# One TensorE signal for a quad of chunks, or two, in a graph kernel of gathers and one-hot sums

## The chip, the cores and the metric

The kernel runs on one core of a Trainium2 chip. The metric is the time of one execution on the device, in microseconds (us). Changes are judged against runs of the kernel before.

## The reference

A block of a graph network on 3125 nodes with 256 features and 53125 directed edges. `src`, `dst` and the edge weights are inputs, so where an edge reads and adds is only known at run time. Cut to what matters:

```python
h = relu(layernorm(x))
x_fwd = segment_sum(w * h[dst, :128], src) / max(degree(src), 1)
x_bwd = segment_sum(w * h[src, 128:], dst) / max(degree(dst), 1)
x = x + concat(x_fwd, x_bwd)

def gat_layer(x, W, b, a, g, beta):
    h = x @ W.T + b
    score = (h @ a[:d])[src] + (h @ a[d:])[dst]
    e = exp(-leaky_relu(score, 0.2))
    return layernorm(segment_sum(e[:, None] * h[dst], src)) * g + beta

h = relu(layernorm(x))
heads = concat([elu(gat_layer(h, ...)) for 8 heads of width 64])   # width 512
x = x + elu(gat_layer(heads, ...))                                 # width 256
```

All of it is in float32.

## The kernel before

Nodes lie in 25 tiles of 128. The kernel sorts the edges by the tile of the node they are summed into, in 464 chunks of 128 edges; two chunks are a group, which belongs to one tile, and four chunks are a quad (116 quads). Sixteen slots hold the rows of sixteen chunks (four quads, a round; 29 rounds).

There are four passes over all chunks. The first (order S) and the second (order D) make the two halves of the weighted mean. The last two are the attention passes "1" (8 heads, rows of 520 numbers) and "2" (one head, rows of 257). In each the same is done for every chunk: GpSimd gathers 128 rows of a table in HBM into the chunk's slot with an indirect DMA (`gather`, L433); TensorE multiplies a one-hot matrix of "edge to lane in its tile" with the rows, so that the rows of one node are added up in PSUM; VectorE adds the finished sum of a group to the accumulator of its tile (`add_group`, L1163, whose add is L1166).

*First and second pass.* ScalarE multiplies the gathered rows by the edge weights (`scale_rows`, L550), VectorE makes a quad's one-hots (`one_hots`, L1158), TensorE sums the quad (`sum_rows`, L809 to L819: four matmuls, two for each group, shown as two records each), VectorE adds (`add_sums`, L1168). Beside 42 of the first 52 quads of a pass, and again in the first pass behind its second cut (`CUT`, quad 56), the sort of the next part of the edges goes on: VectorE makes one-hots of a batch of ten columns of edges (`place_batch`, L1130 to L1137), ScalarE more of them (L538, L541), TensorE 40 matmuls (`place`, L803 to L806), of which the last signals `col_free`, for which the second next batch waits (L1130). The second pass has such batches only until quad 52: what comes behind its second cut is called its tail here.

The signal that binds these is `chunks_summed`, raised by one by TensorE's matmul of every chunk. Three places wait for it: the gather of chunk c for chunk c - 16 (its slot is free), VectorE's one-hots of a quad for the quad four back, and VectorE's adds for their own quad. TensorE in turn waits for `sum_free`, which VectorE's adds raise: a quad is summed when the adds of the quad three back are done.

*Attention passes.* In the order of one turn (quad q), each engine in program order:

- TensorE (`turn`, L955): `source_scores` of quad q + 1 (12 small matmuls, L935; they need the transposed one-hots that ScalarE copied), then `transposed` of quad q + 2 (4 transposes, L925; they need ScalarE's one-hots), then `sums` of quad q (4 matmuls, L950).
- VectorE (`turn`, L1423): `messages` of q (four operations, L1413 in pass 1, L1411 in pass 2), `scores` of q + 1 (L1398, then the leaky ReLU L1402), `add_groups` of q - 1 (L1166).
- ScalarE (`turn`, L650): `weights` of q + 1 (the exponential, L647), the copy of the transposed one-hots of q + 2 (L643), `one_hots` of q + 3 (four of L634, one of L638).
- GpSimd (`gather_layer1`, L447): the gather of chunk c waits in pass 1 for VectorE's message of chunk c - 16, in pass 2 for the sum of its group (`sum_ready`).

TensorE signals four times a quad here: `ohT_psum` after the transposes (ScalarE's copy waits), `ssrc_ready` after the source scores (VectorE's scores wait), and `sum_ready` after each of two groups (VectorE's adds, ScalarE's one-hots, and the gathers of pass 2 wait).

The order on each engine is the order of the program as written. The wait of a gather is the code's line

```python
pool.wait_ge(chunks_summed, phase * CHUNKS + c + 1)
```

where `chunks_summed` begins at 16.

## Time and profile before

| | |
|---|---|
| median of 3 runs | 3293.55 us (3287.83 to 3297.24) |
| the profiled execution | 3294.2 us |
| its span, first to last instruction | 3292.4 us |
| mean granted TensorE clock | 0.825 |
| busy share: PE, DVE, ACT, POOL | 68%, 58%, 53%, 59% |
| gathers | 4 x 464 |

PE is TensorE, PEld its weight loads, DVE VectorE, ACT ScalarE, POOL GpSimd. A line such as L818 is a line of the kernel before. In a row of the timeline the last bracket is how long the engine had been idle before the instruction, and what ended that; "remote" is a releaser that the profile doesn't know, "issue" means that it saw nothing to wait for. The ends of matmuls are modelled. The clock is given as a share of full speed.

### The profile page before, as it was taken

The page shows a single profiled execution, that of the slowest core. Times are in us where ns is not written, and L with a number is a line of the kernel's source. Part 1 is how long each engine was busy: PE and PEld are TensorE (multiplying, and loading weights), DVE is VectorE, ACT ScalarE, POOL GpSimd, SP SyncE. Part 2 cuts the span into 40 slices and gives each one's busy share as a digit, 9 for nine tenths or more (in the row PEclk, how much of TensorE's full clock was granted, in tenths as well). Part 3 has the DMA queues.
Part 4 walks back from the last instruction along what each step waited for, and adds up shares of the span by engine and source line. Part 5 has one row for each costly group of instructions (what it writes and reads, how often), then busy time and mean ns, then how long its engine had stood idle before and what let it go on. Part 6 is the DMA issues. An engine that isn't in the chain of part 4 may idle for free. (4 is left out here: it accounts for less than half of the span.)

```text
span 3292.4 us, 46358 instructions
## 1 busy us (share of the span) xinstructions
PE 2243.2 (68%) x14916; PEld 1669.3 (51%) x14916; DVE 1917.8 (58%) x4213; ACT 1738.7 (53%) x5133; POOL 1928.0 (59%) x1999
## 2 busy tenths in 40 slices
PE   6887778677758877343577777777767566655653
PEld 4785667567747766233343333333335445444542
DVE  8985788577747776222446666666686233333336
ACT  3995677578747776222334444344438344444444
POOL 1006666666666666666635656665645566666664
PEclk8998999799878999555688888888888777777776
DMA  2011111111141112111545656665641333333335
GB/s 60 1 41 40 40 44 43 43 45 45 45 47 44 45 44 53 47 46 47 58 140 160 169 164 173 169 170 157 168 104 33 87 92 89 91 89 90 90 90 77
DMA packets 114882, 270.48 MB, mean 82 GB/s; under 512 B 34543, under 2 KB 51670, under 8 KB 114646
## 3 DMA queue, kind: packets, MB, share of 16 engines
q0 software_dynamic: 89088, 245.53, 30.5%
q1 hardware_dynamic: 25558, 21.98, 2.1%
q8 instruction: 126, 2.06, 0.3%
q14 instruction: 110, 0.90, 0.1%
HBM read 250.96 MB, written 16.42 MB: 81 GB/s over the span
## 5 line engine op out<-in xcount | busy, mean ns | idle before, releaser
L435 POOL DMA_INDIRECT rows_near<-table_a,s_idx_S x464 | 474.1, 1022 | 286.0 <-issue 115.4
L435 POOL DMA_INDIRECT given<-table,s_idx_S x464 | 449.2, 968 | 301.5 <-issue 126.8
L1166 DVE TENSOR_TENSOR work<-work,bank 128x129 f32 (+2 forms) x928 | 391.0, 421 | 362.4 <-remote 163.1
L435 POOL DMA_INDIRECT rows_near<-table,s_idx_S x464 | 446.8, 963 | 252.7 <-issue 127.8
L435 POOL DMA_INDIRECT rows_near<-table_b,s_idx_D x464 | 450.0, 970 | 230.9 <-issue 101.9
L950 PE MATMUL bank<-scratch,oh 128*128 128x512 f32 x928 | 488.1, 675 | 15.9 <-DVE scratch L1413 11.7
L818 PE MATMUL bank<-rows_near,oh 128*128 128x129 f32 x1856 | 331.0, 330 | 246.6 <-issue 179.5
L647 ACT ACTIVATE e_att<-lrelu 128x32 f32<-128x32 f32 (+1 forms) x232 | 49.9, 215 | 740.6 <-DVE lrelu L1402 490.0
L818 PEld LDWEIGHTS bank<-rows_near,oh 128*128 128x128 f32 x1856 | 289.0, 234 | 282.1 <-issue 232.8
L935 PE MATMUL bank<-sort_ring,scratch 128*128 x2784 | 154.0, 169 | 329.4 <-ACT scratch L643 285.2
L538 ACT ACTIVATE scratch<-scratch,given 128x128 f16<-128x128 bf16 x840 | 284.1, 388 | 170.8 <-DVE scratch L1130 146.7
L935 PEld LDWEIGHTS bank<-sort_ring,scratch 128*128 128x128 bf16 x2784 | 135.8, 100 | 455.3 <-issue 436.5
L538 ACT ACTIVATE sort_ring<-sort_ring,given 128x128 f16<-128x128 bf16 x840 | 284.1, 388 | 132.2 <-DVE sort_ring L1130 110.2
L950 PEld LDWEIGHTS bank<-scratch,oh 128*128 128x128 f32 x928 | 193.2, 219 | 224.8 <-issue 204.3
L634 ACT ACTIVATE scratch<-iota_f,s_lo_S 128x128 f32<-128x128 f32 x928 | 293.4, 389 | 18.3 <-PE bank L906 13.7
L803 PE MATMUL bank<-scratch 128*128 128x224 bf16 (+1 forms) x840 | 228.9, 273 | 100.2 <-ACT scratch L538 68.7
L803 PE MATMUL bank<-rows_near,sort_ring 128*128 128x224 bf16 (+1 forms) x840 | 227.7, 271 | 76.2 <-ACT sort_ring L538 50.7
L550 ACT ACTIVATE rows_near<-rows_near,s_w_D 128x128 f32<-128x128 f32 x464 | 163.0, 394 | 216.8 <-DMA rows_near<-table_b,s_idx_D 190.5
L805 PE MATMUL bank<-scratch 128*128 128x224 bf16 (+1 forms) x840 | 229.2, 273 | 15.8 <-issue 15.5
L806 PE MATMUL bank<-scratch 128*128 128x224 bf16 (+1 forms) x840 | 229.3, 273 | 13.6 <-issue 13.6
L804 PE MATMUL bank<-scratch 128*128 128x224 bf16 (+1 forms) x840 | 229.2, 273 | 9.8 <-issue 9.8
L805 PE MATMUL bank<-rows_near,sort_ring 128*128 128x224 bf16 (+1 forms) x840 | 227.6, 271 | 8.3 <-issue 8.1
(222 smaller groups left out, 4799.8 us busy)
## 6 DMA issues: line engine op xcount, KB each, us to landing
rows_near<-table_a,s_idx_S POOLq DMA_INDIRECT x464
rows_near<-table_b,s_idx_D POOLq DMA_INDIRECT x464
rows_near<-table,s_idx_S POOLq DMA_INDIRECT x464
given<-table,s_idx_S POOLq DMA_INDIRECT x464
table<-scratch SPq DMA_DIRECT2D x25, 260.0 KB
table<-scratch SPq DMA_DIRECT2D x25, 128.5 KB, 3.0
xs<-in_x SPq DMA_DIRECT2D x1, 3072.0 KB
out_x<-scratch SPq DMA_DIRECT2D x24, 128.0 KB, 1.7
```

What stands on the lines that cost most here:

```text
L435: nc.gpsimd.indirect_dma_start(out=to, out_offset=None, in_=table[:, :], in_offset=bass.IndirectOffsetOnAxis(ap=s_idx[order][:, c:c + 1], ...
L538: last = nc.scalar.activation(oh_row[n % RING][:, j, :], oh_lane[n % RING][:, j, :], ACT.Copy, scale=row_mid_f[o][:, c:c + 1])
L550: nc.scalar.activation(rows0[:, slot, 0:HALF], rows0[:, slot, 0:HALF], ACT.Copy, scale=s_w[o][:, c:c + 1]).then_inc(rows_scaled, 1)
L634: last = nc.scalar.activation(off_by[:, side + k, :], iota_f[:, 0:P], ACT.Abs, scale=-1.0, bias=s_lo["S"][:, bass.ds(q * QUAD + k, 1)])
L803: nc.tensor.matmul(high, oh_w[n % RING][0][:, j, :], chunks, start=start, stop=stop, skip_group_check=True)
L804: nc.tensor.matmul(low, oh_w[n % RING][1][:, j, :], chunks, start=False, stop=stop, skip_group_check=True)
L805: nc.tensor.matmul(node, oh_node[n % RING][:, j, :], chunks, start=start, stop=stop, skip_group_check=True)
L806: last = nc.tensor.matmul(row, oh_row[n % RING][:, j, :], chunks, start=False, stop=stop, skip_group_check=True)
L818: nc.tensor.matmul(sum0(g), oh[:, slot, :], rows0[:, slot, :], start=(k % GP == 0), stop=(k % GP == GP - 1)).then_inc(chunks_summed, 1)
L935: last = nc.tensor.matmul(bank[2 + u % 2][:, k * heads:(k + 1) * heads], ohT[:, u % 2, k * P:(k + 1) * P], s_parts[:, f, bass.ds(tiles[k / ...
L950: mm = nc.tensor.matmul(bank[4 + u % 2 * 2 + k // GP][:, 0:width], lanes, rows, start=(k % GP == 0), stop=(k % GP == GP - 1))
L1166: v.tensor_add(a, a, psum).then_inc(sum_free[o], 1)
```

## The change

TensorE's signals are made coarser, and every wait for them is rewritten to count quads.

- First and second pass: `chunks_summed` becomes `quads_summed`, raised by the last of a quad's four matmuls. It begins at 4. A gather waits only if it is a quad's first, and then for the whole quad four back; the other three of a quad carry no wait. VectorE's one-hots and adds wait for the same events as before.
- Attention passes: `ohT_psum` and `ssrc_ready` become one signal, `turned_and_scored`, given behind the transposes (of quad q + 2), which come after the source scores (of quad q + 1). So VectorE's scores now wait for the transposes too. `sum_ready` is given once, by the quad's last matmul; VectorE's first add of a quad waits for both groups, and in pass 2 a gather waits for both groups of the quad four back.

No instruction of an engine changes its place. Cut to its core:

```diff
                 for c in range(CHUNKS):
...
-                    pool.wait_ge(chunks_summed, phase * CHUNKS + c + 1)
+                    if c % QUAD == 0:
+                        pool.wait_ge(quads_summed, phase * QUADS + c // QUAD + 1)
                     gather(table, rows0[:, c % SLOTS, 0:HALF], order, c)
...
-                        pool.wait_ge(sum_ready[o], (c - SLOTS) // GP + 1)
+                        pool.wait_ge(sum_ready[o], (c - SLOTS) // QUAD + 1)
...
                 def transposed(q, u):
-                    act.wait_ge(ohT_psum[o], q + 1)
+                    if isinstance(q, int) and q < 2:
+                        act.wait_ge(turned_and_scored[o], q + 1)
+                    else:
+                        act.wait_ge(turned_and_scored[o], q + 2)
...
-                                act.wait_ge(sum_ready[o], i * (2 * UNROLL) + 2 * u)
+                                act.wait_ge(sum_ready[o], i * UNROLL + u)
...
-                    nc.tensor.matmul(sum0(g), oh[:, slot, :], rows0[:, slot, :],
-                                     start=(k % GP == 0), stop=(k % GP == GP - 1)).then_inc(chunks_summed, 1)
+                    last = nc.tensor.matmul(sum0(g), oh[:, slot, :], rows0[:, slot, :],
+                                            start=(k % GP == 0), stop=(k % GP == GP - 1))
+                last.then_inc(quads_summed, 1)
...
-                        if k % GP == GP - 1:
-                            mm.then_inc(sum_ready[o], 1)
+                    last.then_inc(sum_ready[o], 1)
...
-                            source_scores(i * UNROLL + (u + 1), u + 1, tiles[2 * u:2 * u + 2])
-                        if not isinstance(i, int) or q + 2 < QUADS:
-                            transposed(i * UNROLL + (u + 2), u + 2)
+                            last = source_scores(i * UNROLL + (u + 1), u + 1, tiles[2 * u:2 * u + 2])
+                            if not isinstance(i, int) or q + 2 < QUADS:
+                                last = transposed(i * UNROLL + (u + 2), u + 2)
+                            last.then_inc(turned_and_scored[o], 1)
                         sums(q, u)
...
-                dve.wait_ge(chunks_summed, phase * CHUNKS + q * QUAD + QUAD)
+                dve.wait_ge(quads_summed, phase * QUADS + q + 1)
...
-                dve.wait_ge(chunks_summed, SLOTS + phase * CHUNKS + QUAD * (q + 1))
+                dve.wait_ge(quads_summed, SLOTS // QUAD + phase * QUADS + q + 1)
...
-                    dve.wait_ge(ssrc_ready[o], q + 1)
+                    dve.wait_ge(turned_and_scored[o], q + 3)
...
                 def add_groups(q, u, tiles):
+                    dve.wait_ge(sum_ready[o], q + 1)
                     for j in range(2):
-                        dve.wait_ge(sum_ready[o], q * 2 + (j + 1))
```

## Rows read from the trace of the kernel before

**Rows 1.** The page: its span, and the granted TensorE clock in 40 slices.

```profile
span 3292.4 us, 46358 instructions
...
PEclk8998999799878999555688888888888777777776
```

**Rows 2.** Busy time by stage: length, PE, PEld, DVE, ACT, POOL, clock, DMA, GB/s.

```profile
255.50:605.00 349.50, 269.77 (x2185) 229.81 (x2185) 259.37 (x467) 242.61 (x812) 228.29 (x224) 0.92 0.17 43
605.00:962.50 357.50, 258.94 (x2171) 232.17 (x2172) 241.22 (x412) 247.44 (x823) 245.77 (x240) 0.89 0.23 44
962.50:1302.00 339.50, 258.79 (x2118) 224.71 (x2118) 232.00 (x376) 244.53 (x818) 222.27 (x225) 0.91 0.20 45
1302.00:1642.00 340.00, 141.86 (x538) 113.47 (x539) 97.79 (x272) 96.67 (x247) 226.81 (x239) 0.54 0.27 50
1697.00:2439.00 742.00, 558.74 (x2702) 271.55 (x2703) 476.39 (x916) 302.35 (x800) 453.69 (x464) 0.85 0.61 166
2561.00:3240.00 679.00, 408.01 (x2720) 319.70 (x2721) 230.82 (x936) 296.21 (x794) 440.29 (x463) 0.76 0.36 90
```

**Rows 3.** Waits in the tail, 1330 to 1597 us: total, times, longest.

```profile
DVE work L1166 <- remote: 129.8, 27, 8.1
```

**Rows 4.** Timeline of the tail: start, length, instruction, idle before it.

```profile
1392.44 2.40 PE L818 MATMUL bank<-rows_near,oh 128*128 128x129 f32 x8 [1.51 <-issue]
...
1397.30 0.95 POOL L435 DMA_INDIRECT rows_near<-table_b,s_idx_D  x1 [0.30 <-issue]
...
1398.76 0.94 POOL L435 DMA_INDIRECT rows_near<-table_b,s_idx_D  x1 [0.52 <-issue]
...
1400.75 0.72 DVE L1166 TENSOR_TENSOR work<-work,bank 128x129 f32 x2 [7.82 <-remote]
1400.88 0.95 POOL L435 DMA_INDIRECT rows_near<-table_b,s_idx_D  x1 [1.17 <-remote]
...
1401.58 2.06 PE L818 MATMUL bank<-rows_near,oh 128*128 128x129 f32 x8 [6.73 <-issue]
...
1403.70 0.95 POOL L435 DMA_INDIRECT rows_near<-table_b,s_idx_D  x1 [1.88 <-PE bank L818]
...
1456.12 0.95 POOL L435 DMA_INDIRECT rows_near<-table_b,s_idx_D  x1 [0.47 <-remote]
...
1457.55 0.94 POOL L435 DMA_INDIRECT rows_near<-table_b,s_idx_D  x1 [0.48 <-issue]
```

**Rows 5.** Waits before any gather, 100 to 250 us.

```profile
DVE sort_ring L1130 <- PE bank L806: 9.2, 14, 1.0
```

**Rows 6.** Waits in the first attention pass, 1700 to 2430 us.

```profile
DVE score L1398 <- remote: 179.1, 39, 18.0
```

**Rows 7.** Timeline of the first attention pass.

```profile
2009.84 0.45 PE L935 MATMUL bank<-sort_ring,scratch 128*128 x12
...
2015.52 0.95 POOL L435 DMA_INDIRECT given<-table,s_idx_S  x1 [0.30 <-issue]
2018.84 0.19 DVE L1398 TENSOR_TENSOR score<-bank,given 128x32 f32<-128x32 f32 x1 [7.00 <-remote]
```

**Rows 8.** Waits in the second attention pass, 2565 to 3240 us.

```profile
DVE score L1398 <- remote: 303.5, 48, 11.3
...
DVE score L1398 <- PE bank L935: 54.2, 34, 3.3
```

**Rows 9.** Timeline of the second attention pass.

```profile
2709.08 0.16 DVE L1398 TENSOR_TENSOR score<-bank,given 128x4 f32<-128x4 f32 x1 [0.92 <-PE bank L935]
2709.18 0.72 ACT L638 ACTIVATE oh<-scratch,ones 128x512 f32<-128x512 f32 x1
...
2709.96 0.61 PE L925 MATMUL bank<-ident_bf,oh 128*128 128x128 bf16 x4 [0.91 <-ACT oh L638]
...
2710.60 0.60 ACT L643 ACTIVATE scratch<-bank 128x512 bf16<-128x512 bf16 x1 [0.61 <-PE bank L925]
2711.10 1.27 ACT L634 ACTIVATE scratch<-iota_f,s_lo_S 128x128 f32<-128x128 f32 x4
```

More of the change, by code:

```diff
@@ L313, in build @@
         gathered = [sem(f"gathered{i}") for i in range(SLOTS)]
-        chunks_summed = sem("chunks_summed")
+        quads_summed = sem("quads_summed")
         oh_ready = {o: sem(f"oh_ready_{o}") for o in "SD12"}
@@ L317, in build @@
         sum_free = {o: sem(f"sum_free_{o}") for o in "SD12"}
-        ohT_psum = {o: sem(f"ohT_psum_{o}") for o in "12"}
+        turned_and_scored = {o: sem(f"turned_and_scored_{o}") for o in "12"}
         ohT_ready = {o: sem(f"ohT_ready_{o}") for o in "12"}
-        ssrc_ready = {o: sem(f"ssrc_ready_{o}") for o in "12"}
         off_made = {o: sem(f"off_made_{o}") for o in "12"}
@@ L925, in transposed @@
                         last = nc.tensor.transpose(turned[u % 2][:, k * P:(k + 1) * P], upper, ident_bf[:, :])
-                    last.then_inc(ohT_psum[o], 1)
+                    return last
                 def source_scores(q, u, tiles):
@@ L937, in source_scores @@
                                                     start=(f == 0), stop=(f == 2))
-                    last.then_inc(ssrc_ready[o], 1)
+                    return last
                 def sums(q, u):
@@ L949, in sums @@
                             lanes, rows = m[:, 0:P], row_slots(u * QUAD + k, 1)[:, 0, 0:width]
-                        mm = nc.tensor.matmul(bank[4 + u % 2 * 2 + k // GP][:, 0:width], lanes, rows,
-                                              start=(k % GP == 0), stop=(k % GP == GP - 1))
-                        if k % GP == GP - 1:
-                            mm.then_inc(sum_ready[o], 1)
+                        last = nc.tensor.matmul(bank[4 + u % 2 * 2 + k // GP][:, 0:width], lanes, rows,
+                                                start=(k % GP == 0), stop=(k % GP == GP - 1))
+                    last.then_inc(sum_ready[o], 1)
                 def turn(i):
@@ L960, in turn @@
                         if not isinstance(i, int) or q + 1 < QUADS:
-                            source_scores(i * UNROLL + (u + 1), u + 1, tiles[2 * u:2 * u + 2])
-                        if not isinstance(i, int) or q + 2 < QUADS:
-                            transposed(i * UNROLL + (u + 2), u + 2)
+                            last = source_scores(i * UNROLL + (u + 1), u + 1, tiles[2 * u:2 * u + 2])
+                            if not isinstance(i, int) or q + 2 < QUADS:
+                                last = transposed(i * UNROLL + (u + 2), u + 2)
+                            last.then_inc(turned_and_scored[o], 1)
                         sums(q, u)
-                transposed(0, 0)
-                transposed(1, 1)
-                source_scores(0, 0, tile_numbers(mybir.EngineType.PE, "S", TILE_AT, 2))
+                transposed(0, 0).then_inc(turned_and_scored[o], 1)
+                transposed(1, 1).then_inc(turned_and_scored[o], 1)
+                source_scores(0, 0, tile_numbers(mybir.EngineType.PE, "S", TILE_AT, 2)).then_inc(turned_and_scored[o], 1)
                 turn(0)
@@ L1019, in _ @@
             dve.sem_inc(consts_made, 1)
-            dve.sem_inc(chunks_summed, SLOTS)
+            dve.sem_inc(quads_summed, SLOTS // QUAD)
             dve.sem_inc(col_free, RING)
```

## The prediction

> **What bounds the kernel now.** I read the page first [rows 1]: a span of 3292.4 us in an execution of 3294.2 us, and a granted TensorE clock that sits at half speed in slices 17 to 20 and well under full after them, which says that TensorE waits. So I cut the span into stages [rows 2]: the first pass until its second cut (349.5 us), its rest (357.5), the second pass while edges are still being placed (339.5), its tail (340.0), and the two attention passes (742 and 679).
>
> In each stage I ask how fast the gathers alone could go. Between two gathers that nothing delays GpSimd idles 0.30 us [rows 4], so a stage's floor is its GpSimd busy time plus 0.30 us for each gather [rows 2]. Tail: 226.8 + 239 x 0.30 = 298.5 us of 340.0. First attention pass: 453.7 + 464 x 0.30 = 592.9 of 742. Second: 440.3 + 139.2 = 579.5 of 679. The first three stages: 228.3 + 245.8 + 222.3 + 689 x 0.30 = 903 of 1046.5. So 41, 149, 99 and 143 us are stalls of the gathers, on a ring of 16 slots. Something behind the ring is late.
>
> What is late? In the tail, VectorE's adds of finished sums idled 129.8 us in 27 waits put down to "remote", a releaser the profile can't name [rows 3]. They wait for TensorE's signal alone, and for their own previous add. The timeline shows such a wait [rows 4]: TensorE's eight matmuls (a chunk is two records) ran from 1392.44 us to 1394.84, and TensorE did nothing until 1401.58; VectorE had been idle 7.82 us when it started at 1400.75. All matmuls issued so far had ended 5.9 us before. **The signal of a finished matmul arrives microseconds late.** In those microseconds GpSimd issued gathers back to back (1397.30, 0.30 us after the one before), and the wait ended just when GpSimd had to pause (0.52, then 1.17 us idle). Elsewhere in the tail GpSimd goes in lockstep, 0.47 or 0.48 us idle before each gather [rows 4], 0.17 more than undisturbed. In the stretch before any gather runs, the same handover from TensorE to VectorE costs 9.2 us in 14 waits, 1.0 at most [rows 5]. My reading: while GpSimd issues gathers, TensorE's signals queue up, and get through mainly when GpSimd pauses.
>
> Both attention passes show it. In the first, `score` waited 179.1 us in 39 "remote" waits; the small matmuls it needs began at 2009.84 and take under half a microsecond, the last gather before the pause was issued at 2015.52, and `score` began at 2018.84 after 7.00 us idle [rows 6, 7]. In the second it is 303.5 us in 48 waits [rows 8]. GpSimd then runs out of slots and TensorE idles.
>
> **The change, part by part.** The instructions of the engines stay in their order. TensorE's signals fall from four to one per quad in the first two passes (928 to 232) and from four to two in the attention passes (928 to about 466).
>
> *Signals themselves.* Eight records with four signals take 2.06 us at half clock [rows 4], about 0.22 a start, so a signal shows no time of its own: 0. The Trainium skill (TensorE: Matmul & The Clock Gate, "The cost: per-tile semaphore tail") says increments serialise at about 26.3 ns each; by it the 1,158 removed would give an estimated 30 us at most, and none where TensorE waits. No row here shows that cost by itself, and the rule has no delay of microseconds in it, which this trace does have.
>
> *Tail of the second pass.* At four signals per quad and four gathers per quad, one signal gets through per pause of 0.17 us. With one signal a quad, GpSimd pauses once in four: 60 quads x 0.17 = 10 us of stall remain of 41. I take **-30**; ends 0 and -41.
>
> *Coarser wait of the gathers.* The first gather of a quad now waits for the fourth chunk of the quad four back, not its first: up to three quarters of 2.06, 1.5 us, where it was the wait that ended last. Chunks two to four lose their waits. A row speaks against a cost: the gather at 1403.70, released by L818, began after all eight records of 1401.58 had ended (1403.64) [rows 4]. Late signals come in bunches. I take 0 in the tail; ends 0 and 1.5 us x 116 quads = +174 a pass.
>
> *First three stages.* A batch of 40 placing matmuls with one signal of its own sits in most steps, and VectorE's next batch waits for that signal, which the change leaves alone. VectorE is busy 259 of 349.5 us there, TensorE 270 [rows 2]. I take **-5** of 143.
>
> *First attention pass.* Signals per quad go from four to two, half a signal per gather: a held signal has fewer in front of it. The stall to be had is 149 us. TensorE's work is 558.7 us / 116 = 4.8 us a quad and VectorE's 4.1, against the gathers' 5.1 [rows 2], so none forbids a gain. But what holds the signals is GpSimd's gathers, and these remain as dense. I take a quarter: **-35**; ends +20 and -130.
>
> *Second attention pass.* The same quarter of 99 is -25. Against it: the scores' signal now comes after the transposes too, which wait for ScalarE's one-hots. A row shows the distance: `score` at 2709.08, one-hots at 2709.18 for 0.72, the transposes at 2709.96 for 0.61 [rows 9], so 1.5 us later. It costs where VectorE waits for exactly that, 34 times [rows 8]: 51 us if nothing absorbs it. Since the ring and not the single quad bounds the pass I charge 15: **-10**; ends +80 and -80. In the first attention pass `score` comes after four messages of VectorE that cover most of it.
>
> *VectorE's adds* wait for both groups of a quad at once; their sums are a quad old by then: 0.
>
> Sum: -30 - 5 - 35 - 10 = -80, so 3294.2 - 80 = **3214 us**. The profiled execution is 0.65 us above the median of the runs (3293.55), so nothing is to be corrected.
>
> **The rivals.** *The hold hardly counts the signals.* It ends when GpSimd pauses and lets all through, however many there are. For it: the long waits shown end with GpSimd's long pauses, not its short ones [rows 4, 7]. Then only the tail gains, the attention passes do not, and the later scores signal takes something back: 3294 - 30 + 15 = 3279. Chance 0.22.
>
> *The queue was all of it.* With fewer signals than pauses nothing piles up, and the passes go near their floors: -38 in the tail, -110 and -70 in the attention passes, -35 before: 3041. For it: lockstep one to one in the tail. Against it: the batch signal of the first stages is already rare. Chance 0.15.
>
> *Slower: the merged signal.* The signal of scores and transposes closes a loop: `score` and its leaky ReLU, weights, the copy of the transposes (0.60), one-hots (1.27 and 0.72 us on ScalarE), transposes (0.61), `score` [rows 9]. It decides once that loop with a held signal exceeds the 5.1 us of four gathers; with some 0.6 us for the three small ones that comes to 3.8 us without a hold, so a mean hold over 1.3 us per quad is enough. If it takes 1.5 us at half of the 232 attention quads (174 us) and pauses of the ring hide 80 of that, then with the tail's gain the time is 3294 + 174 - 80 - 30 = 3358. Chance 0.10; and 0.05 that the coarser gather wait costs half a quad's matmuls (1 us) at 100 of 232 quads, 3294 + 100 - 45 = 3349.
>
> *Nothing moves*: the signals still arrive with the next pause of GpSimd, and all that goes is a price per signal, for which no row shows more than nothing: 3294. Chance 0.04. (By the skill's rule quoted above this case would give 3264.)
>
> **How the numbers follow.** Forecast 0.44, rivals 0.22, 0.15, 0.15 (two slower ones) and 0.04. A measurement of this kernel tells about 0.3%, or 10 us, from no change. The first rival lies at the edge of that: I give 0.15 of its 0.22 to faster and 0.07 to no change. Faster 0.44 + 0.15 + 0.15 = 0.74, plus 0.02 from slower ones that gain elsewhere: 0.76. Same 0.07 + 0.04 = 0.11. Slower 0.13. The forecast's own terms reach from 3294 - 41 - 15 - 90 - 50 = 3098 to 3294. The range 3100 to 3310 leaves out most of the full relief (0.13) and the slower cases beyond 3310 (0.09).
>
> **What would show it.** In the changed profile: the tail near 310 us, GpSimd's 0.47 us pauses rarer and single; VectorE's "remote" waits of the adds well under 129.8 us; `score`'s 179.1 and 303.5 us reduced by a quarter or more; the granted clock at half speed over fewer slices. Direct waits of `score` for TensorE should grow in the second attention pass, now ended by the transposes. It is wrong if the attention passes keep 742 and 679 us, or if the second one grows.

## The result, and the profile after

The changed kernel takes 3301.43 us (median of 18 runs, 3287.80 to 3309.49), the kernel before beside it 3290.25 us (18 runs, 3278.86 to 3297.24). The ratio is 1.0029, with a 95% interval of 1.0016 to 1.0042. The forecast was 3214 us, 80 us less than before; not only was nothing gained, some 10 us were lost. All lines of this document are lines of each run's own kernel, so that one statement can have several numbers: the adds are L1166 before and L1170 in the changed kernel.

The page of the changed kernel, its span and the granted clock, to be laid beside [rows 1]:

```profile
span 3289.2 us, 46126 instructions
...
PEclk8997999899978998555688889888887777777776
```

Busy time by stage over the same windows and in the same columns as [rows 2]:

```profile
255.50:605.00 349.50, 273.35 (x2200) 233.81 (x2201) 263.89 (x483) 243.87 (x815) 232.51 (x229) 0.90 0.17 44
...
1302.00:1642.00 340.00, 174.93 (x548) 119.03 (x547) 96.63 (x278) 99.73 (x255) 229.09 (x243) 0.55 0.28 51
1697.00:2439.00 742.00, 563.71 (x2704) 271.52 (x2704) 476.28 (x918) 294.70 (x792) 464.68 (x461) 0.85 0.60 166
2561.00:3240.00 679.00, 431.89 (x2727) 332.89 (x2725) 240.07 (x948) 293.65 (x798) 439.32 (x464) 0.76 0.37 90
```

In each window GpSimd gets through nearly the same number of gathers as before (243 in the tail for 239, 461 for 464, 464 for 463), at the same clocks (0.55, 0.85, 0.76 for 0.54, 0.85, 0.76). Nothing sped up anywhere. These windows can't show where the 10 us went: the profiled execution of the changed kernel took 3291.18 us, 3 us less than the profiled one of before.

The waits in the tail, 1330 to 1597 us, in total, times and longest; first GpSimd's own in the kernel before, beside the line of [rows 3]:

```profile
POOL rows_near L435 <- issue: 33.3, 108, 0.5
...
POOL rows_near L435 <- remote: 30.9, 47, 3.2
...
POOL rows_near L435 <- PE bank L818: 23.1, 33, 2.1
```

and the changed kernel:

```profile
DVE work L1170 <- remote: 128.0, 16, 19.0
...
POOL rows_near L434 <- issue: 54.5, 179, 0.3
POOL rows_near L434 <- remote: 28.8, 9, 4.7
```

This is the reading of the whole case. The change did what it says: a gather has to wait for a signal only once a quad, and GpSimd's waits for TensorE fell from 80 (47 remote, 33 direct) to 9. The **sum** of GpSimd's idle time hardly moved, 83.3 us for 87.3. Both windows hold 188 gathers, and 188 x 0.30 = 56.4 us of it is there without any delay, so the delays are 27 us for 31. VectorE's adds tell the same, 128.0 us of remote waits in 16 for 129.8 in 27, the longest now 19.0 us for 8.1. Fewer and longer waits, nearly the same time.

The changed kernel's timeline in the tail shows one such wait. To read it one has to count quads: the first matmuls below are those of quad 70, the records of 1390.28 and 1392.77 those of quad 72, the adds of 1398.62 those of quad 70, and the gather of 1398.75 is the first of quad 74, which waits for quad 70.

```profile
1381.72 2.06 PE L821 MATMUL bank<-rows_near,oh 128*128 128x129 f32 x8 [5.20 <-DVE work L1170]
...
1390.28 2.03 PE L821 MATMUL bank<-rows_near,oh 128*128 128x129 f32 x6 [0.60 <-issue]
...
1392.77 0.80 PE L821 MATMUL bank<-rows_near,oh 128*128 128x129 f32 x2 [0.46 <-issue]
...
1394.75 0.94 POOL L434 DMA_INDIRECT rows_near<-table_b,s_idx_D  x1 [0.30 <-issue]
...
1397.28 0.40 ACT L550 ACTIVATE rows_near<-rows_near,s_w_D 128x128 f32<-128x128 f32 x1 [0.83 <-DMA rows_near<-table_b,s_idx_D]
1398.62 0.72 DVE L1170 TENSOR_TENSOR work<-work,bank 128x129 f32 x2 [7.39 <-remote]
1398.75 0.94 POOL L434 DMA_INDIRECT rows_near<-table_b,s_idx_D  x1 [3.06 <-remote]
...
1399.45 2.06 PE L821 MATMUL bank<-rows_near,oh 128*128 128x129 f32 x8 [5.89 <-DVE work L1170]
```

The last row confirms the count: quad 73 may be summed when the adds of quad 70, three back, are done. So quad 70 was summed at 1383.78 us, and its one signal let VectorE and GpSimd go on at 1398.62 and 1398.75, **14.84 us** later. TensorE had summed two further quads meanwhile, the last at 1393.57, and GpSimd had been out of slots since 1395.69. The trace also keeps the times at which a semaphore was raised. This one rose at 1398.49, 1398.59 and 1398.68, for quads 70, 71 and 72, and then at 1401.53, 0.02 us behind the end of quad 73.

Counted in this way over quads 58 to 107, the adds of a quad begin 10.3 us (median) behind its matmuls in the changed kernel, and 14.0 and 12.0 us in two profiles of the kernel before. Single quads reach 16.7 us in the changed kernel and 19.6 in the kernel before. Behind some long stops of GpSimd (3.06 us at 1398.75) two of the next quads are handed over in 0.15 us, and then the delay is back; behind others (4.24 us at 1477.37) it doesn't go away at all. One signal a quad is held about as long as four were.

In the kernel before, the adds of 1400.75 in [rows 4] are by the same count those of quad 69, summed at 1384.58, 16.17 us earlier. Its semaphore rose nine times between 1403.45 and 1403.79. But it also rose seven times between 1386.5 and 1391.48, while the gathers came 0.30 us apart, each signal 11 to 14 us late. So a pause isn't the only time in which signals pass.

In the attention passes (1700 to 2430 and 2565 to 3240 us, two answers) `score` waits as follows, for 179.1 us in 39 waits [rows 6], and for 303.5 in 48 and 54.2 in 34 [rows 8]:

```profile
DVE score L1402 <- remote: 169.7, 38, 14.4
```

```profile
DVE score L1402 <- remote: 241.8, 56, 14.9
...
DVE score L1402 <- PE bank L929: 121.1, 53, 2.4
```

In the second pass 62 us of remote waits went, and 67 us of direct waits for the transposes came. The pass is as long as before.

### The profile page after: what moved, and what is told of

Same layout as the page of the kernel before. It is cut to its first block and busy times, and to the rows that moved or that the text cites. A ratio compares the mean times of both kernels' runs of the same rounds, so it can differ in the third digit from the quotient of the medians.

```text
span 3289.2 us, 46126 instructions
## 1 busy us (share of the span) xinstructions
PE 2307.1 (70%) x14916; PEld 1694.7 (52%) x14916; DVE 1919.3 (58%) x4213; ACT 1730.4 (53%) x5133; POOL 1941.4 (59%) x1999
## 5 line engine op out<-in xcount | busy, mean ns | idle before, releaser
L434 POOL DMA_INDIRECT rows_near<-table,s_idx_S x464 | 455.0, 981 | 279.3 <-issue 128.3
L1170 DVE TENSOR_TENSOR work<-work,bank 128x129 f32 (+2 forms) x928 | 390.1, 420 | 368.0 <-remote 176.2
L821 PE MATMUL bank<-rows_near,oh 128*128 128x129 f32 x1856 | 367.2, 337 | 225.8 <-DVE work L1170 76.1
L821 PEld LDWEIGHTS bank<-rows_near,oh 128*128 128x128 f32 x1856 | 296.9, 231 | 289.1 <-issue 187.6
L806 PE MATMUL bank<-scratch 128*128 128x224 bf16 (+1 forms) x840 | 230.3, 274 | 94.3 <-ACT scratch L538 54.1
L806 PE MATMUL bank<-rows_near,sort_ring 128*128 128x224 bf16 (+1 forms) x840 | 229.1, 273 | 67.4 <-ACT sort_ring L538 39.5
L808 PE MATMUL bank<-scratch 128*128 128x224 bf16 (+1 forms) x840 | 230.6, 274 | 16.5 <-issue 16.5
L808 PE MATMUL bank<-rows_near,sort_ring 128*128 128x224 bf16 (+1 forms) x840 | 228.9, 273 | 13.7 <-issue 13.7
L807 PE MATMUL bank<-scratch 128*128 128x224 bf16 (+1 forms) x840 | 230.7, 275 | 6.6 <-issue 6.5
L807 PE MATMUL bank<-rows_near,sort_ring 128*128 128x224 bf16 (+1 forms) x840 | 229.2, 273 | 7.8 <-issue 7.8
## 6 DMA issues: line engine op xcount, KB each, us to landing
out_x<-scratch SPq DMA_DIRECT2D x24, 128.0 KB, 1.7
```

The costliest lines, as they stand in the source:

```text
L434: nc.gpsimd.indirect_dma_start(out=to, out_offset=None, in_=table[:, :], in_offset=bass.IndirectOffsetOnAxis(ap=s_idx[order][:, c:c + 1], ...
L806: nc.tensor.matmul(high, oh_w[n % RING][0][:, j, :], chunks, start=start, stop=stop, skip_group_check=True)
L807: nc.tensor.matmul(low, oh_w[n % RING][1][:, j, :], chunks, start=False, stop=stop, skip_group_check=True)
L808: nc.tensor.matmul(node, oh_node[n % RING][:, j, :], chunks, start=start, stop=stop, skip_group_check=True)
L821: last = nc.tensor.matmul(sum0(g), oh[:, slot, :], rows0[:, slot, :], start=(k % GP == 0), stop=(k % GP == GP - 1))
L1170: v.tensor_add(a, a, psum).then_inc(sum_free[o], 1)
```

## The experiments

From here on there are three theories. **A**: TensorE's signals are held while GpSimd issues gather upon gather, and all that are pending pass in a pause of GpSimd that is long enough; their number is worth nothing. (The seven raises above already speak against its second clause as it stands.) **B**, the forecast's: they stand in a queue, and each costs its turn. **C**: the ring is bound by the latency from a freed slot to summed rows. The runs lay on several chips, so every ratio is one to the kernel before on the same chip. On most its median was 3290 to 3294 us; where it was 3325 to 3331, this is said. Stage lengths are from the start of a stage's first gather to that of its last; those of before are 706, 680, 741 and 679 us.

### Which part of the change costs

**The first two passes alone**: the diff of the change without its attention part.

> Only the first two passes changed: one signal for the four sums of a quad, and the three waits that follow (gathers at a quad's first chunk); the attention passes as before. Theory A (TensorE's signals are held while GpSimd issues gather upon gather and all let go in GpSimd's next pause, however many there are): the two passes keep their length, 0 +- 4 us against before. Theory B (the signals stand in a queue of their own and each costs its turn, 1856 - 464 = 1392... of these 928 sums' signals become 232): the vector engine's remote waits in the second pass's tail fall and the run is 10 to 40 us faster. If the +0.3% of the whole change sits here (a first gather of a quad that waits for the quad's last sum instead of its first), this kernel is 8 to 10 us slower.

Measured: 3295.89 us, ratio 1.0010 (0.9999 to 1.0021). Nothing gained, as A has it; a loss can't be told from none. (The expectation's count is muddled: 928 signals become 232.)

**The attention passes alone**: the rest of the diff.

> Only the attention passes changed: one signal for turned and scored, one for the four sums; the first two passes as before. Theory A: the length stays or grows by the merged signal alone, since the score waits for the four transposes behind the 12 small matmuls (up to 1.5 us where a quad's cycle is bound by it): 0 to +12 us, and if the whole change's +0.3% sits here it is +8 to +10. Theory B (queue): 10 to 45 us faster, the score's remote waits in both passes down by a quarter or more.

Measured: 3298.81 us, ratio 1.0029 (1.0015 to 1.0042). A loss as large as that of the whole change is here. B's gain of 10 us or more isn't. Then its two halves.

**The merged signal of turned and scored alone**, as in the change's diff from `ohT_psum` to `turned_and_scored`:

> Of the change only the merged signal for turned and scored in both attention passes; the sums keep a signal a pair and the first two passes are as before. If the +0.3% of the attention passes' part comes from the score waiting for the transposes, this kernel is 1.002 to 1.004 of before, with the score's direct waits for TensorE in the second attention pass near 121 us as in the whole change (54 before). If it comes from the coarser signal of the sums (the second pass's gathers, the one-hots and the adds wait for a quad's fourth sum), it is within 0.0015 of before.

Measured: 3355.48 us, ratio 1.0086 (1.0071 to 1.0102) on a chip where before takes 3325 us. That is more than both halves together had cost elsewhere, so it was run once more:

> The merged signal for turned and scored alone, once more. If its 1.0086 holds whatever the chip, 1.007 to 1.010 again, and the parts of the change don't add up. If it was the chip (before takes 3290 us on it, not 3325), and the parts add: both attention parts 1.0029 less the sums' signal alone 1.0017 give 1.001, range 0.999 to 1.004.

Measured: 3305.50 us, ratio 1.0034 (1.0019 to 1.0048). So on a chip like those of the other parts it costs what the whole change costs. In the profile of the run on the slower chip the first attention pass takes 782 us, in this one 745; why stays open.

**The sums' signal alone**:

```diff
-                        if k % GP == GP - 1:
-                            mm.then_inc(sum_ready[o], 1)
+                    last.then_inc(sum_ready[o], 1)
```

> Of the change only the sums' signal of the attention passes: one a quad in place of one a pair, and the three waits that follow; everything else as before. If parts add up, this is the whole of both attention parts (1.0029) less the merged signal's (1.0086): 0.993 to 0.996 of before, the second attention pass shorter by 5 us or more. If the merged signal's +0.9% was particular to its combination or to the chip, this kernel is 0.998 to 1.003.

Measured: 3298.01 us, ratio 1.0017 (1.0004 to 1.0030). Not the gain that I had worked out from runs of two chips: I had subtracted ratios of different chips. The halves measured 0.34% and 0.17%, both together 0.29%; the intervals don't tell whether they add up. Each half costs a little, and none gives anything. In the profiles the first attention pass is 745 us in the changed kernel, 751 with the attention part alone and 754 with the sums' signal, for 741 and 734 in two profiles of before; the second stays between 677 and 680 us in all of them. That the loss sits in the first is likely, but with 7 us between two profiles of one kernel it isn't shown.

### Does the number of signals count

Five times as many, the added ones on a semaphore that nobody waits for:

```diff
                         last = nc.tensor.transpose(turned[u % 2][:, k * P:(k + 1) * P], upper, ident_bf[:, :])
+                        if k < QUAD - 1:
+                            last.then_inc(nobody, 1)
...
+                            if k * 3 + f < QUAD * 3 - 1:
+                                last.then_inc(nobody, 1)
```

and the same for `high`, `low` and `node` in `place`.

> The kernel before with about twice to three times as many signals of TensorE: every transpose, every matmul of the source scores and every matmul of the placement also counts up a semaphore that nobody waits for (3 + 11 more per quad in each attention pass, 12 more for every 4 placement steps or 48 per batch). Theory A (what is pending goes together, the number does not matter): 3290 +- 10 us, the vector engine's remote waits in the tail (129.8) and at the score (179.1, 303.5) within 15%. Theory B (a queue, each signal its turn of about 0.3 us while gathers are issued): hundreds of us slower, and the remote waits at the score at least double. By the page rule of about 26 ns a signal on TensorE itself (the Trainium skill, TensorE page, per-tile semaphore tail) the 14 more per quad x 232 quads are 3248 x 0.026 = about 85 us more TensorE time in the attention passes.

Measured: 3318.68 us, ratio 1.0070 (1.0052 to 1.0087). The added signals are 14 x 232 = 3248 in the attention passes and 3 x 1680 = 5040 in the placement (the expectation's count for the placement was too low), beside some 2000 there were. The tail has none of them, since the placing ends before it; the attention passes have 14 more in each quad, 18 for 4. The waits of the tail (1330 to 1597) as a control, and of both attention passes (1712 to 2442 and 2587 to 3252, since they begin later here):

```profile
DVE work L1171 <- remote: 138.0, 23, 18.3
```

```profile
DVE score L1403 <- remote: 177.2, 34, 16.9
```

```profile
DVE score L1403 <- remote: 273.3, 43, 12.1
```

177 for 179.1, and 273 for 303.5, where the signals are 4.5 times as many; 138 for 129.8 in the control. B is dead: a queue with a turn for each signal would have multiplied them. An added signal costs at most 28 us / 8288 = 3.4 ns on the mean. The Trainium skill (TensorE: Matmul & The Clock Gate, "The cost: per-tile semaphore tail") gives about 26.3 ns each; by that the 3248 in the attention passes would be an estimated 85 us. The two passes grew by 8 and 4 us, so most of that price doesn't show here, and the measurement decides.

### Is it the gathers that hold the signals

Pass 1 and both attention passes get their rows by plain DMAs from SyncE, behind the same waits. The rows are 128 consecutive ones of the table, not the edges' own: this kernel leaves the gathering out. The second pass keeps its gathers and is the control.

```diff
+            def plain(table, to, c):
+                t = c % T
+                sp.dma_start(to, table[t * P:(t + 1) * P, :]).then_inc(gathered[c % SLOTS], 16)
```

> The gathers of pass 1 and of both attention passes are replaced by plain DMAs of 128 consecutive rows, issued from SyncE behind the same waits; the rows are not the gathered ones, so the output is not the reference's. Pass 2 keeps its gathers on GpSimd. Theory A (what holds TensorE's signals is GpSimd issuing gathers): in the three moved stages the remote waits of the vector engine all but vanish (under 30 us each, direct waits on TensorE or on data take their place), and the first attention pass falls from 741 to 570-620 us, the second from 679 to 450-600; pass 2, the control, keeps its 680 us and its tail's remote waits of about 130. Theory B (the queue of signals itself): the remote waits stay, since TensorE makes as many signals. Theory C (the loop is bound by the latency from a freed slot to landed rows): stage lengths stay near those of before with the waits on DMA in place of the remote ones.

Measured: 2598.42 us, ratio 0.7894 (0.7883 to 0.7905), 692 us less, of a kernel whose engines compute all that they did before. Busy time over the four stages of transfers:

```profile
255.00:791.00 536.00, 477.26 (x4345) 444.48 (x4346) 491.53 (x873) 483.51 (x1634) 0.00 (x0) 0.96 0.21 58
793.00:1470.00 677.00, 414.21 (x2668) 342.08 (x2667) 330.98 (x653) 340.39 (x1062) 448.59 (x465) 0.73 0.23 47
1527.00:2098.00 571.00, 505.10 (x2792) 251.19 (x2792) 498.94 (x970) 306.64 (x815) 10.34 (x11) 0.98 0.70 216
2142.00:2543.00 401.00, 329.64 (x2889) 271.17 (x2887) 248.71 (x1014) 323.22 (x847) 7.85 (x14) 0.98 0.56 160
```

536 for 706 us, 571 for 741, 401 for 679, and the control 677 for 680. The waits in the control's tail (1130 to 1425), and all that `score` has left in the second attention pass:

```profile
DVE work L1178 <- remote: 133.2, 18, 19.7
```

```profile
DVE score L1410 <- PE bank L947: 54.8, 54, 5.6
```

Not one remote wait of `score` is left in either attention pass. Where GpSimd gathers, the adds wait 133 us for "remote" with the same number of signals; where it doesn't, TensorE's signals arrive. In the second attention pass `score` begins 0.04 us (median) behind the last of its small matmuls; in the kernel before it is 1.6 us, and over 4 us in 39 of 116 quads. This shows that GpSimd's indirect DMAs do it. Whether it is the issuing on GpSimd or the transfers that it makes isn't told apart, since the replacement changes both; nor is the whole gain the signals', since four gathers also take GpSimd 5.0 us a quad and plain DMAs don't (a floor of 580 to 593 us for an attention pass by [rows 2], and the first pass and both attention passes now lie below it).

### How long a pause, and how often

GpSimd writes one element of a tile of its own and waits for it, n times behind every gather or every fourth:

```diff
+                if c % 4 == 3:
+                    for _ in range(4):
+                        link(nc.gpsimd.memset(pause_at[:, :], 0.0))
```

> The kernel before, with GpSimd writing one element of a tile of its own behind every gather, and waiting for that write before it goes on. Theory A with the length of the pause as what counts (what is pending passes when the pause is over some 0.35 us): if the added write and wait make the gap of 0.30 us between gathers some 0.5 us or more, the vector engine's remote waits at the score (179.1 and 303.5) and in the tail (129.8) fall by half or more, and each stage comes near 4 x (0.95 + gap) us per quad x 116: with a gap of 0.5 some 670 us, against 706, 680, 741, 679, so 50 to 100 us faster in all; with a gap over 0.7 the gathers themselves bound it and it is slower. If instead a busy GpSimd of any kind holds the signals (the write included), the remote waits stay and the run is slower by what is added, 1856 x 0.1 to 0.2 us less what pauses hide: +50 to +200 us. Theory B (queue): as the last.

> The kernel before, with four such writes and waits of GpSimd behind every fourth gather (one pause a quad, as long as the four of a quad in the run with a pause behind each gather). Theory A: what is pending passes once a quad, remote waits at the score below before's but above those with a pause behind each gather; time between the two. If writes keep the signals held as gathers do: remote waits as before, the run slower by about as much as the one with a pause behind each gather.

> The kernel before with two of GpSimd's writes and waits behind every fourth gather, in place of four (four made a gap of 1.15 us once a quad and left the first attention pass 14 of 179 us of remote waits). Theory A: the gap becomes 0.5 to 0.8 us; if that is enough for what is pending to pass, remote waits go as with four writes and each stage is 116 x 0.3 to 0.6 = 35 to 70 us shorter where GpSimd's own cadence bounds it (the first attention pass): 20 to 120 us faster than before. If the gap is too short for it, the run is that of before plus at most 116 x 4 x 0.3 = 140 us: same to 2% slower, remote waits as before.

> The same with one write a quad: a gap of about 0.36 us once a quad, as behind each gather in the run with a write each, where the remote waits stayed (180 and 290 us at the score). Theory A with a threshold between 0.36 and 1.15 us: remote waits as before, time within -0.3 to +1% of before.

Measured, all on chips where before takes 3325 to 3331 us; the gap is from the end of one gather to the start of the next in GpSimd's timeline, the waits are `score`'s remote ones in windows in the two attention passes (1760 to 2420 in all; 2650 to 3230 for the first and last line, 2680 to 3230 for the others):

| pause | gap, us | ratio | remote waits, us |
|---|---|---|---|
| one write, each gather | 0.36 | 1.0206 (1.0178 to 1.0234) | 180.1, 289.5 |
| one write, each quad | 0.36 | 1.0232 (1.0207 to 1.0256) | 161.8, 284.0 |
| two writes, each quad | 0.85 | 1.0106 (1.0081 to 1.0131) | 156.7, 222.3 |
| four writes, each quad | 1.15 | 0.9908 (0.9882 to 0.9933) | 14.2, 227.3 |

GpSimd with a long pause, and the waits of `score` in that run's first attention pass:

```profile
2106.64 0.95 POOL L436 DMA_INDIRECT rows_near<-table,s_idx_S  x1 [0.30 <-issue]
2107.57 0.53 POOL L442 MEMSET pause_at<- 1x1 f32 x4
2108.72 0.99 POOL L436 DMA_INDIRECT given<-table,s_idx_S  x1 [0.62 <-issue]
```

```profile
DVE score L1402 <- DMA given<-table,s_idx_S: 83.4, 48, 2.6
...
DVE score L1402 <- remote: 14.2, 2, 8.5
```

One stretch of 1.15 us a quad without a gather takes the remote waits of this pass from about 180 us to 14, with TensorE's signals untouched; `score` now waits for rows. In the tail (1330 to 1597) the adds have no remote wait left:

```profile
DVE work L1170 <- PE bank L822: 186.5, 46, 5.3
```

47 of the 50 quads 58 to 107 are now handed over in 0.15 us. That pass is no shorter for it, 699 us for 680. And in the second attention pass most of the remote waits stay, 227.3 us, although the stretch is the same; it takes 699 us for 679. (The 680 and 679 are from a chip on which the kernel before is some 37 us faster in all.) So 1.15 us is enough in these two stages and not in the second attention pass, and why is open.

A gap of 0.36 us, even behind every gather, lets nothing more through than 0.30. So GpSimd made slower can make the kernel faster. Whether its delay has to be one piece isn't shown, because the runs with longer pauses also gather more slowly: without other waits a quad takes 5.06 us with one write, 5.24 with a write each gather, 5.55 with two and 5.84 with four, and the remote waits of the first attention pass are 157 to 180 us up to 5.55 and 14 at 5.84. The same 0.85 us spread over the four gathers was not run. My expectation for the run with a write each gather took a pause of half a microsecond to be enough, which its gap never reached. That one short write a quad costs 2.3%, more than the 116 x 4 x 0.06 us it adds, I can't explain.

**With the pause, is the change worth something?** The changed kernel with four writes a quad, on another chip with the slower before:

> The changed kernel with four writes a quad, as the run of the kernel before with them (that was 0.991 of before, 0.9882 to 0.9933). Theory A: with the signals let through once a quad their number is worth nothing either, so the same 0.991 within 0.003; a merged signal that lets the score wait for the transposes costs up to 10 us more. If the change's saving was only hidden by the held signals, this is another 20 to 40 us faster, 0.980 to 0.985.

Measured: 3305.60 us, ratio 0.9939 (0.9922 to 0.9957), against 0.9908 (0.9882 to 0.9933) without the change. No hidden saving came out.

**Fewer slots**, so that GpSimd must wait oftener: each gather waits for the quad three back (below), or two back, not four.

```diff
-                    pool.wait_ge(chunks_summed, phase * CHUNKS + c + 1)
+                    pool.wait_ge(chunks_summed, phase * CHUNKS + c + 5)
```

With two quads it is `c + 9`; in the attention passes the 16 slots of the wait become 12 and 8.

> The kernel before, but every gather waits until the quad three before its own is done (sums in the first two passes, messages in the first attention pass, sums in the second), not four: the ring is used with 12 slots, GpSimd must pause oftener. Theory A: TensorE's signals pass at each of these pauses, so the remote waits at the score fall although the buffering is smaller; the stages keep their length or shrink (0 to 60 us each at most), the run is 0 to 150 us faster. Rival C (what bounds is the latency from a freed slot to summed rows, ring size over latency): with 12 of 16 slots the stages grow by up to a third, 200 to 900 us slower.

> The same with a lead of two quads (8 of the 16 slots). Theory A: GpSimd pauses in every quad; remote waits fall further, but a quad's chain (gather 5.0 us, landing, scaling or score and messages, sums of 4 to 5 us) no longer fits in two quads of gathers everywhere: between 100 us faster and 400 us slower. Rival C: twice the time per quad of before, over 1000 us slower in all.

Measured: 0.9967 (0.9951 to 0.9982) and 1.0061 (1.0039 to 1.0084), before at 3331 us. Half of the ring taken away costs 0.6%; with a quarter taken away the kernel is a little faster. That is the end of C: latency round a ring would have cost a third and the double. With two quads the remote waits of `score` in the second attention pass (2650 to 3230) are gone too, its place taken by rows that come late:

```profile
DVE score L1398 <- DMA given<-table,s_idx_S: 178.5, 45, 5.3
DVE score L1398 <- DMA rows_near<-table,s_idx_S: 147.4, 44, 5.2
...
DVE score L1398 <- remote: 7.2, 5, 2.6
```

### A version that beats both kernels

The pause only where it pays, in the first attention pass: `if o == "1" and c % QUAD == QUAD - 1:` ahead of the four writes in `gather_layer1`.

> The kernel before with four of GpSimd's writes and waits behind every fourth gather in the first attention pass alone. Theory A: the pause let every signal through there (remote waits at the score 14 of 179 us) and brought that pass to some 711 us, while in the other stages, whose own stalls came to 100 to 126 us, it cost 10 to 20 us each: so this kernel gains the first and does not pay the rest, 25 to 45 us faster than before (0.986 to 0.992), and faster than with pauses in all stages (0.991). If the gain lay elsewhere, 0.995 to 1.005.

Measured: 3254.49 us, ratio **0.9875 (0.9859 to 0.9891)**, 36 us less than before. With a pause behind every eighth gather in its place:

> As the run with pauses in the first attention pass alone (0.9875), but a pause behind every eighth gather there. If GpSimd's own cadence bounds that pass (116 x (4 x 1.25 + 1.1) = 708 us, as measured), half the pauses take 116 x 1.1 / 2 = some 60 us off it until something else bounds it: 0.970 to 0.982. If signals held for a quad longer cost that again (score needs the signal of every quad), the pass comes back to 720 to 740 us: 0.990 to 1.000, remote waits at the score back to 50 to 150 us. I take the second as likelier.

Measured: 3300.20 us, ratio 1.0023 (1.0008 to 1.0038). `score`'s waits over 1715 to 2400 us, once a quad and every other quad:

```profile
DVE score L1402 <- DMA given<-table,s_idx_S: 89.6, 54, 3.2
...
DVE score L1402 <- DMA rows_near<-table,s_idx_S: 59.8, 43, 2.9
```

```profile
DVE score L1402 <- remote: 178.5, 44, 12.5
```

With one pause a quad the pass takes 708 us, which is GpSimd's own cadence: on the mean 4 gathers of 1.01 us, three gaps of 0.31 and one of 1.14 make 6.12 us a quad. With half of the pauses it takes 746, and the remote waits are all back. Either a pause must come in every quad, or the mean cadence must be slow enough (it is 5.42 us a quad here, where nothing else waits); the run doesn't tell the two apart. Adding the sums' coarser signal:

> Both of the two: the sums' coarser signal in the attention passes and GpSimd's pauses in the first of them. If both help on their own and the coarser signal works through the second attention pass, the ratios multiply: 0.981 to 0.988. If the coarser signal's gain was in the first attention pass, through held signals, the pause has already taken it: as the pause alone.

Measured: 3248.86 us, ratio 0.9870 (0.9855 to 0.9885), not to be told from the pause alone. The kernel before, unchanged, among these runs:

> The kernel before, unchanged, for its profile on the same chip as the three others: 1.000 within 0.003. Its four stages of gathers show what of the later runs' lengths belongs to the chip: if the chip makes the +35 us by which the kernel before is slower here, the stages of before sum to some 2830 to 2850 us in place of 2806.

Measured: 1.0000 (0.9985 to 1.0015), stages 703, 680, 734 and 678 us. So stages of one kernel differ by up to 7 us between two profiles. It didn't lie on a chip with the slower before, and where those lose their 35 us stays open.

## Why the prediction was wrong, point by point

- **What bounds the kernel**: right. Signals of finished matmuls arrive late while GpSimd gathers, and the price is large, with the 692 us of the run without gathers as a bound from above, in which the gathers' own cadence is contained.
- **"TensorE's signals queue up", so that fewer of them wait less**: the step that failed. The row that carried it was the lockstep of 0.47 us gaps [rows 4], read as one signal per pause, so that a quarter of the signals would need a quarter of the pauses. The short gaps did become rare (80 waits for TensorE to 9), and the time reappeared in long ones: 27 us of delays for 31. What the runs showed in its place is a delay in time, in the tail 10.3 us (median of 50 quads) with one signal a quad and 12.0 and 14.0 with four, and waits that 4.5 times the signals in the attention passes don't lengthen. The trace of before already had it: the semaphore rose nine times in 0.34 us shortly behind the 7.82 us wait, and seven times between gathers only 0.30 us apart. The delay itself was underrated too: "ended 5.9 us before" is right of the last matmuls issued, but those that the adds waited for had ended 16.17 us before.
- **Tail, -30**: 0 (the whole second pass takes 683 us in the profile, for 680). First three stages, -5: 0 (the first two passes alone measured +0.1%, interval down to 0).
- **Coarser wait of the gathers, 0**: right in the first two passes.
- **First attention pass, -35**: +4 in the profile of the changed kernel, +9 and +13 with parts of the change, of which 7 us can be scatter. "A held signal has fewer in front of it" was the argument, and the run with 4.5 times the signals here showed no longer waits.
- **Second attention pass, -10**: 0. The direct waits for the transposes appeared, as forecast (121 us for 54), and cost the pass nothing; the merged signal's +0.3% may be in the first attention pass, where I had it covered by the messages, but no run shows that.
- **Signals themselves, 0**: right within 3.4 ns x 1158 = 4 us; eight records take 2.06 us with four signals [rows 4] and with one (the rows of 1381.72 and 1399.45 above).
- **The rivals**: "the hold hardly counts the signals" came nearest to the mechanism, at 0.22 where it should have stood first; its 3279 had the tail's gain of 30 us, which by its own logic it should not have had. Without it it says 3309, for 3301 measured. The measured time lies inside the range, but near its upper end and not by the forecast's mechanism. The lower end was also added up from -90 and -50 for the attention passes, where the parts had said -130 and -80. The chance of faster, 0.76, was the real error: four of five cases shared one unshown step, that signals compete.

## What to carry to other kernels

If an engine waits long for a finished producer, first count which matmul it waits for: with queues between the engines it is not the last one in the timeline. Then count the waits as well as their sum. In this kernel making the signals fewer changed how many waits there were, not their time. Before the signals are made coarser, make them many on a semaphore that nobody reads: one run prices a signal. And where GpSimd gathers without a break beside engines that hand over to each other, try a pause in every round of gathers, and measure it stage by stage, since it helped one stage here and is not seen to help the others.

## What the runs showed of the hardware that I had not expected

- A stream of indirect DMAs from GpSimd goes with completion signals of TensorE that arrive 10 us and more late in half of the tail's quads or more (14.84 us in the timeline above), and plain DMAs of the same size from SyncE don't hold them, though they move the rows faster (216 for 166 GB/s in the first attention pass).
- The delay hardly depends on the number of signals. Held signals can pass together, three in 0.19 us or nine in 0.34, but also one by one between gathers that are 0.30 us apart.
- A gap of 0.36 us between gathers lets no more through than one of 0.30. One of 1.15 us in every quad ends the late signals in the tail and nearly all in the first attention pass, and leaves most of the remote waits in the second (227.3 us, for 289.5 over the same window with a write each gather). Longer gaps aren't always enough: at 1380.76 us in the changed kernel, 1.4 us after the last gather had been issued, one signal passed and the next, of matmuls that had ended at 1371.62, only at 1384.32. What exactly releases a signal, and whether the length of a pause or the mean rate of the gathers decides, stays open.
- Idle stretches put into the engine that issues the transfers, in one of four passes, shortened the kernel by 1.25%.
